# Four edits to the schedule of a two-layer graph and expert network: where a pair is added to X, which small loads come first, and the order of the first prologue

## The chip, the cores and the metric

The kernel runs on one core of a Trainium2 chip. The metric is the device time in microseconds (us). Before the change the median of three runs is 4302.01 us (4301.11 to 4304.52).

## The reference

Four residual layers work on x, 2048 rows of 128 channels. Every layer reads the row-normalised x and its result is added to x:

```python
x = x + _L0_gnn_ref(_layernorm(x), ...)   # masked attention over the graph, 8 heads of 16 channels, with a curvature bias
x = x + _L0_ffn_ref(_layernorm(x), ...)   # product keys: top 16 of a table for each row and head, then causal attention
x = x + _L1_gnn_ref(_layernorm(x), ...)   # graph attention:
#   Wh = einsum('nf,hfd->hnd', x, W_heads); e = leaky_relu(Wh.a1 [:, None] + Wh.a2 [None, :])
#   att = softmax(where(adj > 0, e, NEG)); feat = elu(att @ Wh) for 8 heads of 128; feat @ W_out + b_out
x = x + _L1_ffn_ref(_layernorm(x), ...)   # 16 experts, the best two by gate weighted, then a row norm
```

## The kernel before

X stays on the chip (16 tiles of 128 rows). Three stages follow one another, each with a barrier at its end; every engine has its own written-out instruction list and the order is set by semaphores alone.

**curvature_keys_and_attention** does the first two layers. A unit is 16 nodes with their 8 heads, a tile of X has 8 units. Its prologue loads some 30 constants through SP's queue (L421 to L452), normalises X, and makes `hT`, `vals` (L522, copied at L705), the two products with `al_w` and `ar_w` (L528, L532), `el_wide` (L709), `er_rows` (L712) and, on VectorE, `el_cols` (L838, L843). SP waits for `er_rows` (L440), stores it as the last rows of `bias_rhs` (L442), and then issues the loads of the key and attention weights (L443 to L452). TensorE waits for all of these before the first `logits_of` (L550). After that the units run: score matmuls, a maximum on VectorE (`max_of`, L862), exp on ScalarE (L732), four turns and products (L557, L565). One tile later the rows of the tile before choose their keys (`choose`, L905 to L966): 16 gathers a unit on GpSimd (L506), which VectorE adds two units later (L991). In the first unit with a choice (t = 1, k = 0) the order on TensorE is query product (L641), `logits_of` for the next unit, similarity product (L650); on ScalarE `qT` copy (L774), `relu_of`, `diff_of`, `sim` copy (L784); on VectorE `max_of`, then `choose`.

**graph_attention** is the third layer: 128 units u (8 heads of 16 tiles), and pairs g = u // 2 of two tiles of one head. VectorE makes the scores of the next unit (`scores`: L1394, L1398, L1404) and one reciprocal (L1443); ScalarE the exp of the next unit between the second and third of its four copies (L1331, L1340); TensorE turns the unit four blocks at a time (L1240) and lays the products of the pair before between them (`weigh`, L1253). At the end of every even unit 2m TensorE makes `project(m - 3)` (L1264). In VectorE's list an even turn 2m of the loop is: scores(2m + 1), reciprocal, `head_of(m - 2)` (L1412, L1415), `add_to_x(m - 3)` (L1431, waits for `project(m - 3)`). An odd turn 2m + 1 is: scores(2m + 2), reciprocal, `feat_of(m - 2)` (L1421, waits for `exp_below(m - 2)` of ScalarE, L1345, and for `project(m - 3)`). The reciprocals of a pair go through DRAM and come back on all partitions: two stores (L1186), a wait for both, one load (L1190), all on SP's queue in order. In head 0 VectorE also scales a tile of the mask in every unit (L1381); in four units of a head TensorE makes the values of the next head (L1219). The stage's prologue loads five constants on one semaphore; TensorE waits for all five, makes 16 products of one column each (L1198), and only then turns the normalised X (L150).

**experts** loads nine constants on one semaphore, turns X, waits for all nine, makes the gate products (L1546), chooses two experts on VectorE (L1635 to L1661), and runs 64 up and down products.

Of the kernel before, what the change touches and what calls it, by code (L numbers as in the profile page):

```python
# [7 lines left out]
P = 128  # L8
T = N // P
H = 8  # L10
CH = 512
# [179 lines left out]
def curvature_keys_and_attention(nc, ins, X, ident, big_ident, psL, psT, psV, psO, keysT_out, values_out, adj_out):  # L191
# [28 lines left out]
    with ExitStack() as ctx:  # L220
# [195 lines left out]
        with nc.Block() as block:  # L416
            @block.sync
            def _(sp):
# [33 lines left out]
                sp.dma_start(ahead[:, :], ins["c_ahead"][:, 0, 0:P]).then_inc(at_in, 16)  # L452

# [57 lines left out]
            def _(pe):  # L511
# [3 lines left out]
                for c in range(NC):  # L515
                    nc.tensor.matmul(psL[:, c * CH:(c + 1) * CH], w_t, xT[:, c * CH:(c + 1) * CH],
                                     start=True, stop=True).then_inc(prep_mm, 1)
                for q in range(4):
# [6 lines left out]
                pe.wait_ge(weights_ready, 2)  # L525
                pe.wait_ge(prep_copied, 8)
                for c in range(NC):
                    nc.tensor.matmul(psL[:, c * CH:(c + 1) * CH], al_w, hT[:, c * CH:(c + 1) * CH],  # L528
                                     start=True, stop=True).then_inc(prep_mm, 1)
                for c in range(NC):  # L530
                    pe.wait_ge(prep_copied, 9 + c)
                    nc.tensor.matmul(psL[:, c * CH:(c + 1) * CH], ar_w, hT[:, c * CH:(c + 1) * CH],  # L532
                                     start=True, stop=True).then_inc(prep_mm, 1)
# [97 lines left out]
                def tile(t, s1, last, choosing, adding):  # L631
                    for k in range(H):
# [10 lines left out]
                        if s1:  # L643
# [54 lines left out]
            def _(act):  # L698
                norm.scalar(act)
                for c in range(NC):  # L700
                    act.wait_ge(prep_mm, c + 1)
                    nc.scalar.copy(hT[:, c * CH:(c + 1) * CH], psL[:, c * CH:(c + 1) * CH]).then_inc(prep_copied, 1)
                for q in range(4):
                    act.wait_ge(prep_mm, 4 + q + 1)
                    nc.scalar.copy(vals[:, 4 * q:4 * q + 4, :].rearrange("p s c -> p (s c)"),  # L705
                                   psT[:, q % 2, :]).then_inc(prep_copied, 1)
                for c in range(NC):
                    act.wait_ge(prep_mm, 8 + c + 1)
                    nc.scalar.mul(el_wide[:, c * CH:(c + 1) * CH], psL[:, c * CH:(c + 1) * CH],  # L709
                                  1.0 - SLOPE).then_inc(prep_copied, 1)  # L710
                act.wait_ge(prep_mm, 16)
                nc.scalar.copy(er_rows[:, :], psL[:, :]).then_inc(prep_copied, 4)  # L712
                act.wait_ge(cols_ready, 2)
                act.wait_ge(prep_copied, 16)
# [53 lines left out]
                def tile(t, s1, last, choosing, adding):  # L768
                    for k in range(H):
                        v = H * (t - 1) + k  # L770
                        ahead = k < KU - 1 or not last
                        if choosing:
                            act.wait_ge(qT_done, v + 1)
                            nc.scalar.copy(qT[:, :], psT[:, 0, 0:P]).then_inc(qT_copied, 1)  # L774
                        if s1 and ahead:
# [3 lines left out]
                        if choosing:  # L779
# [36 lines left out]
                diff_of(0, 0)  # L816
# [7 lines left out]
            def _(dve):  # L824
# [12 lines left out]
                dve.wait_ge(prep_copied, 12)  # L837
                nc.vector.tensor_tensor(el_wide.rearrange("p (u i) -> p u i", i=G),  # L838
                                        el_wide.rearrange("p (u i) -> p u i", i=G),
                                        node_pick[:, :].unsqueeze(1).to_broadcast([P, UNITS, G]),  # L840
                                        ALU.mult).then_inc(el_mult, 1)
                dve.wait_ge(el_mult, 1)
                nc.vector.tensor_reduce(el_cols[:, :], el_wide.rearrange("p (u i) -> p u i", i=G),  # L843
                                        mybir.AxisListType.X, ALU.add).then_inc(cols_ready, 1)
# [166 lines left out]
                def tile(t, s1, last, choosing, adding):  # L1011
                    for k in range(H):
# [16 lines left out]
                        if s1 and ahead:  # L1029
# [9 lines left out]
                        else:  # L1039
                            attend_now()  # L1040
                        if summing is not None:
# [19 lines left out]
                turn_adj(0)  # L1061
                dve.wait_ge(keys_in, 64)
# [6 lines left out]
def graph_attention(nc, ins, X, ident, psL, psT, psV, psO, adj_kept, s2_kept, rinv_kept):  # L1069
# [9 lines left out]
    with ExitStack() as ctx:  # L1079
# [33 lines left out]
        consts_in = sem("consts_in")  # L1113
        adj_in = [sem(f"adj_in{g}") for g in range(4)]
# [41 lines left out]
        with nc.Block() as block:  # L1156
            @block.sync
            def _(sp):
                sp.dma_start(w_all[:, :], ins["W_all"]).then_inc(consts_in, 16)
                sp.dma_start(w_heads_t, ins["W_heads_t"]).then_inc(consts_in, 16)  # L1160
                sp.dma_start(a_cols, ins["a_cols"]).then_inc(consts_in, 16)
# [33 lines left out]
            def _(pe):  # L1195
                pe.wait_ge(consts_in, 80)
                for n in range(2 * H):
                    last = nc.tensor.matmul(psO[:, n:n + 1], w_heads_t[:, n % H, :], a_cols[:, n:n + 1],  # L1198
                                            start=True, stop=True)
# [31 lines left out]

                for c in range(NC):
# [132 lines left out]
            def _(dve):  # L1365
# [6 lines left out]
                def add_bias():  # L1372
# [425 lines left out]
```

## Time and profile before

| | |
|---|---|
| median of three runs | 4302.01 us |
| the profiled execution | 4302.53 us |
| its span, first to last instruction | 4300.8 us |
| busy over the span | PE 80%, VectorE 77%, ScalarE 53%, GpSimd 48% |
| mean granted TensorE clock | 0.919 of full speed |
| first stage, prologue and units | about 0 to 3002 us |
| graph attention | 3002 to 4034 us |
| experts | 4034 to 4300 us |

The profile names engines PE (matmul), PEld (weight load), DVE (VectorE), ACT (ScalarE), POOL (GpSimd) and SP (the DMA queue's engine). A line of the timeline has the start, the duration, the engine, the line of code, the operation, output and input with their shapes, how many instructions were merged, and in brackets how long the engine was idle before and what ended that. A matmul of 32-bit data shows as two instructions.

### The profile page before, as it was taken

How to read it: one execution, taken by the hardware profiler on the slowest of the kernel's cores; microseconds unless marked ns; L12 is line 12 of the kernel's file. 1: busy time of each engine (PE TensorE's matmuls, PEld its weight loads, DVE VectorE, ACT ScalarE, POOL GpSimd, SP SyncE). 2: the span in 40 equal slices, each digit the busy share in tenths (PEclk: the TensorE clock that was granted, in tenths of full speed). 3: DMA queues.
4: the chain of work that ended last, by engine and by line, in shares of the span. 5: the costliest groups of instructions: out<-in, count | busy, mean ns of one | idle time of the engine just before them, and what ended most of it. 6: DMA issues, size and time to landing. Idle time of an engine off the chain costs nothing. (4 is left out here: it accounts for less than half of the span.)

```text
span 4300.8 us, 61129 instructions
## 1 busy us (share of the span) xinstructions
PE 3427.1 (80%) x19161; PEld 2640.9 (61%) x19288; DVE 3315.0 (77%) x10546; ACT 2259.3 (53%) x3612; POOL 2047.6 (48%) x2052
## 2 busy tenths in 40 slices
PE   6867778777777788888888989665878888887799
PEld 4645555555555566666666666544667777776676
DVE  2679889898898898988988889774777777777434
ACT  5645455555555565565655656322555555555333
POOL 0377777777777777777767667661000000000000
PEclk9988889899999999999999999777899999999899
DMA  2244444455455555555556555553322122222200
GB/s 76 60 128 118 134 141 131 145 143 154 149 155 161 162 166 175 176 173 175 187 172 199 177 166 194 185 176 136 102 29 25 14 29 29 29 29 9 46 3 8
DMA packets 217422, 501.28 MB, mean 117 GB/s; under 512 B 63676, under 2 KB 115072, under 8 KB 210816
## 3 DMA queue, kind: packets, MB, share of 16 engines
q0 software_dynamic: 98304, 268.57, 21.4%
q1 hardware_dynamic: 118796, 228.80, 19.1%
q8 instruction: 156, 2.56, 0.3%
q14 instruction: 166, 1.36, 0.2%
HBM read 470.64 MB, written 26.41 MB: 116 GB/s over the span
## 5 line engine op out<-in xcount | busy, mean ns | idle before, releaser
L506 POOL DMA_INDIRECT ck_ring<-in_tables,ck_rows x2048 | 2047.4, 1000 | 884.0 <-issue 750.6
L991 DVE SCALAR_TENSOR_TENSOR ck_part<-ck_ring,ck_norm_w,ck_part 128x256 f32<-128x256 f32 x1792 | 770.0, 477 | 61.2 <-DVE ck_rows L966 41.7
L565 PE MATMUL psV<-ck_vals,ck_probsT 128*128 128x128 f32 x4096 | 556.5, 285 | 109.0 <-ACT ck_probsT L740 102.5
L550 PE MATMUL psL<-ck_bias_rhs,ck_bias_w 110*128 110x512 f32 x1024 | 573.4, 643 | 87.1 <-ACT ck_bias_rhs L727 38.5
L565 PEld LDWEIGHTS psV<-ck_vals,ck_probsT 128*128 128x128 f32 x4096 | 504.2, 197 | 157.8 <-ACT ck_probsT L740 89.0
L1253 PE MATMUL psL<-ga_probsT,ga_vals 128*128 128x256 f32 x2048 | 531.5, 407 | 0.7 <-ACT ga_probsT L1340 0.7
L740 ACT COPY ck_probsT<-psT 128x512 f32<-128x512 f32 x512 | 281.9, 587 | 446.4 <-PE psT L557 445.3
L1240 PE MATMUL psT<-ident,ga_probs 128*128 128x128 f32 x2048 | 300.2, 281 | 188.8 <-ACT ga_probsT L1340 187.6
L1253 PEld LDWEIGHTS psL<-ga_probsT,ga_vals 128*128 128x128 f32 x2048 | 399.5, 205 | 51.7 <-ACT ga_probsT L1340 0.9
L1240 PEld LDWEIGHTS psT<-ident,ga_probs 128*128 128x128 f32 x2048 | 248.3, 145 | 242.2 <-issue 214.5
L1331 ACT ACTIVATE ga_probs<-ga_probs,ga_neg_mx 128x2048 f32<-128x2048 f32 x128 | 256.4, 2003 | 225.4 <-DVE ga_neg_mx L1404 225.2
L1340 ACT COPY ga_probsT<-psT 128x512 f32<-128x512 f32 x512 | 280.3, 584 | 177.8 <-PE psT L1240 177.6
L583 PE MATMUL psL<-ck_keysT,ck_at_qT 128*128 128x512 f32 (+3 forms) x640 | 271.2, 556 | 91.0 <-DVE ck_neg_mx L866 90.9
L602 PE MATMUL psO<-ck_at_probsT,ck_values 128*128 128x128 f32 x2176 | 308.0, 291 | 41.5 <-ACT ck_at_probsT L747 41.5
L602 PEld LDWEIGHTS psO<-ck_at_probsT,ck_values 128*128 128x128 f32 x2176 | 276.1, 201 | 71.2 <-ACT ck_at_probsT L747 71.2
L550 PEld LDWEIGHTS psL<-ck_bias_rhs,ck_bias_w 110*128 110x128 f32 x1024 | 213.6, 209 | 166.4 <-issue 146.3
L557 PE MATMUL psT<-ident,ck_probs 128*128 128x128 f32 x2048 | 307.5, 286 | 3.1 <-ACT ck_sim L784 2.7
L1394 DVE SCALAR_TENSOR_TENSOR ga_probs<-ga_s_rows,ga_s_cols,ga_s_slope 128x2048 f32<-128x2048 f32 x128 | 300.3, 2346 | 0.6
L1398 DVE CUSTOM_DVE_ANT_0 ga_probs<-ga_probs,ga_adj_neg 128x2048 f32<-128x2048 f32 x128 | 292.7, 2286 | 5.5
L862 DVE CUSTOM_DVE_ANT_0 ck_relu_part<-psL,ck_relu_part 128x2048 f32<-128x2048 f32 x128 | 292.8, 2288 | 0.5 <-issue 0.5
L747 ACT COPY ck_at_probsT<-psT 128x512 f32<-128x512 f32 (+3 forms) x320 | 158.9, 524 | 206.0 <-PE psT L590 206.0
L732 ACT ACTIVATE ck_probs<-ck_relu_part,ck_neg_mx 128x2048 f32<-128x2048 f32 x128 | 257.8, 2014 | 16.0 <-DVE ck_neg_mx L866 16.0
(210 smaller groups left out, 5455.7 us busy)
## 6 DMA issues: line engine op xcount, KB each, us to landing
ck_ring<-in_tables,ck_rows POOLq DMA_INDIRECT x2048, 2.8
ck_adj_raw<-in_adj SPq DMA_DIRECT2D x16, 1024.0 KB, 9.0
adj_scratch<-ck_adj_neg SPq DMA_DIRECT2D x16, 512.0 KB, 10.4
values_scratch<-ck_values_tile SPq DMA_DIRECT2D x128, 64.0 KB, 1.7
keysT_scratch<-ck_keys_tile SPq DMA_DIRECT2D x128, 64.0 KB, 1.9
ck_keysT<-keysT_scratch SPq DMA_DIRECT2D x8, 1024.0 KB
ck_values<-values_scratch SPq DMA_DIRECT2D x8, 1024.0 KB
ga_adj_neg<-adj_scratch SPq DMA_DIRECT2D x16, 512.0 KB, 11.6
```

The source lines that it names most:

```text
L506: pool.indirect_dma_start(ring[:, slot, :], None, ins["tables"], bass.IndirectOffsetOnAxis(rows[:, k, s:s + 1], axis=0)).then_inc(got[(u * ...
L550: last = nc.tensor.matmul(psL[:, c * CH:(c + 1) * CH], bias_w[:, :], bias_rhs[:, k % 2, c * CH:(c + 1) * CH], start=False, stop=True)
L557: last = nc.tensor.transpose(psT[:, q % 2, s * P:(s + 1) * P], probs[:, j * P:(j + 1) * P], ident[:, :])
L565: last = nc.tensor.matmul(psV[:, k % 2, :], probsT[:, q % 2, s, :], vals[:, j, :], start=(j == 0), stop=(j == T - 1))
L602: last = nc.tensor.matmul(psO[:, P:2 * P], values[:, j, :], at_probsT[:, q % 2, j % 4, :], start=(j == 0), stop=(j == blocks(v) - 1))
L740: nc.scalar.copy(probsT[:, q % 2, :, :].rearrange("p s c -> p (s c)"), psT[:, q % 2, :]).then_inc(probsT_ready, 1)
L862: nc.vector.tensor_tensor_reduce(out=logits[:, :], in0=psL[:, :], in1=relu_part[:, :], scale=1.0, scalar=-3.0e38, op0=ALU.add, op1=ALU.max ...
L991: done.append(c.did(nc.vector.scalar_tensor_tensor(part[:, s % 2, :], ring[:, slot, :], norm_w[:, s:s + 1], part[:, s % 2, :], ALU.mult, A ...
L1240: last = nc.tensor.transpose(psT[:, q % 2, s * P:(s + 1) * P], probs[:, u % 3, j * P:(j + 1) * P], ident[:, :])
L1253: last = nc.tensor.matmul(out, vals[:, k % 2, j, :], probsT[:, g % 2, j, :, :].rearrange("p h i -> p (h i)"), start=(j == 0), stop=(j == T ...
L1394: nc.vector.scalar_tensor_tensor(probs[:, u % 3, :], s2_rows[:, k % 2, :], s1_cols[:, t, k:k + 1], s2_slope[:, k % 2, :], ALU.add, ALU.max ...
L1398: nc.vector.tensor_tensor_reduce(out=probs[:, u % 3, :], in0=probs[:, u % 3, :], in1=adj_neg[:, t, :], scale=1.0, scalar=-3.0e38, op0=ALU.add,
```

## The change

- **graph_attention, loop:** `add_to_x(m - 3)` moves from the even turn 2m to the odd turn 2m + 1, behind `feat_of(m - 2)`.
- **graph_attention, prologue:** the two loads for the score weights come first and have a semaphore of their own; the 16 products of one column become 8 of two columns. The other three loads are waited for before the first values, and before the bias is added.
- **experts:** the gate's weights, bias and numbering are loaded first, on their own semaphore; TensorE waits for the other six loads only after the gate products, VectorE before the gates.
- **First prologue:** the `al_w` and `ar_w` products come ahead of the `vals` products; ScalarE copies in that order and makes `diff_of(0, 0)` between the second and third copy of `vals`; SP's wait for `er_rows` and the two stores move behind the weight loads; VectorE turns the mask before it makes `el_cols`.
- **First unit with a choice:** the similarity product, its copy and `choose` come ahead of the logits, the relu and the maximum of the next unit.

```diff
@@ curvature_keys_and_attention, SP
-                sp.wait_ge(prep_copied, 13)
-                for b in range(2):
-                    sp.dma_start(bias_rhs[KW:KB, b, :], er_rows[0:H, :]).then_inc(er8_in, 16)
                 sp.dma_start(wq[:, :, :], ins["Wq_pk"]).then_inc(keys_in, 16)
...
                 sp.dma_start(ahead[:, :], ins["c_ahead"][:, 0, 0:P]).then_inc(at_in, 16)
+                sp.wait_ge(prep_copied, 12)
+                for b in range(2):
+                    sp.dma_start(bias_rhs[KW:KB, b, :], er_rows[0:H, :]).then_inc(er8_in, 16)
@@ TensorE: the two score products, then vals
+                pe.wait_ge(weights_ready, 2)
+                pe.wait_ge(prep_copied, 4)
+                for c in range(NC):
+                    nc.tensor.matmul(psL[...], al_w, hT[...], start=True, stop=True).then_inc(prep_mm, 1)
+                for c in range(NC):
+                    pe.wait_ge(prep_copied, 5 + c)
+                    nc.tensor.matmul(psL[...], ar_w, hT[...], start=True, stop=True).then_inc(prep_mm, 1)
                 for q in range(4):
-                    pe.wait_ge(prep_copied, 4 + q)
+                    if q >= 2:
+                        pe.wait_ge(prep_copied, 11 + q)
@@ TensorE, tile
+                        opening = choosing and not adding and k == 0
-                        if s1:
+                        if s1 and not opening:
                             if k < KU - 1:
                                 logits_of(t, k + 1)
...
+                        if opening:
+                            logits_of(t, k + 1)
@@ graph_attention
-                pe.wait_ge(consts_in, 80)
-                for n in range(2 * H):
-                    last = nc.tensor.matmul(psO[:, n:n + 1], w_heads_t[:, n % H, :], a_cols[:, n:n + 1],
-                                            start=True, stop=True)
+                pe.wait_ge(heads_in, 32)
+                both = a_cols.rearrange("f (a h) -> f h a", h=H)
+                for h in range(H):
+                    last = nc.tensor.matmul(psO[:, 0:2 * H].rearrange("c (a h) -> c h a", h=H)[:, h, :],
+                                            w_heads_t[:, h, :], both[:, h, :], start=True, stop=True)
...
-                    if u % 2 == 0 and 0 <= u // 2 - 3 < GROUPS:
+                    if u % 2 == 1 and 0 <= u // 2 - 3 < GROUPS:
                         add_to_x(u // 2 - 3)
@@ experts
-                pe.wait_ge(consts_in, 144)
+                pe.wait_ge(gate_in, 48)
                 pe.wait_ge(norm.xT_done, T // 4)
...
                 last.then_inc(gates_done, 1)
+                pe.wait_ge(consts_in, 96)
```

## Rows read from the trace of the kernel before

**Rows 1.** Windows, graph attention: length, then busy by engine, granted clock, DMA share.

```profile
3095.00:4017.00 922.00, 744.67 (x4272) 649.51 (x4272) 664.14 (x961) 538.30 (x808) 0.00 (x0) 0.94 0.23 25
3059.00:3112.00 53.00, 47.09 (x275) 38.42 (x273) 41.94 (x61) 34.37 (x55) 0.00 (x0) 1.00 0.32 35
```

**Rows 2.** Waits, 3100 to 4010: who waited for whom, total, times, longest.

```profile
DVE X L1431 <- PE psV L1264: 241.3, 59, 6.2
```

**Rows 3.** Timeline, graph attention, units 112 to 115.

```profile
3903.96 1.11 PE L1240 MATMUL psT<-ident,ga_probs 128*128 128x128 f32 x8 [2.76 <-ACT ga_probsT L1340]
...
3911.53 0.42 DVE L1431 TENSOR_TENSOR X<-X,psV 128x256 f32<-128x256 f32 x1 [4.74 <-PE psV L1264]
...
3911.81 1.06 PE L1240 MATMUL psT<-ident,ga_probs 128*128 128x128 f32 x8 [0.32 <-ACT ga_probsT L1340]
3911.86 2.35 DVE L1394 SCALAR_TENSOR_TENSOR ga_probs<-ga_s_rows,ga_s_cols,ga_s_slope 128x2048 f32<-128x2048 f32 x1
...
3917.11 2.35 DVE L1394 SCALAR_TENSOR_TENSOR ga_probs<-ga_s_rows,ga_s_cols,ga_s_slope 128x2048 f32<-128x2048 f32 x1
...
3919.97 1.06 PE L1240 MATMUL psT<-ident,ga_probs 128*128 128x128 f32 x8 [2.77 <-ACT ga_probsT L1340]
...
3922.50 0.29 DVE L1415 TENSOR_SCALAR ga_belowT<-ga_headT 128x256 f32<-128x256 f32 x1
...
3925.89 0.42 ACT L1345 ACTIVATE ga_belowT<-ga_belowT 128x256 f32<-128x256 f32 x1
3926.14 1.06 PE L1240 MATMUL psT<-ident,ga_probs 128*128 128x128 f32 x8 [0.32 <-ACT ga_probsT L1340]
```

**Rows 4.** Timeline: starts of units 3, 4, 7 and 127, mask scaling, values.

```profile
3062.86 1.06 PE L1240 MATMUL psT<-ident,ga_probs 128*128 128x128 f32 x8 [0.77 <-ACT ga_probsT L1340]
...
3069.02 1.06 PE L1240 MATMUL psT<-ident,ga_probs 128*128 128x128 f32 x8 [0.77 <-ACT ga_probsT L1340]
...
3069.60 0.69 DVE L1381 TENSOR_SCALAR ga_adj_neg<-ga_adj_neg 128x2048 bf16<-128x2048 bf16 x1
...
3088.47 1.04 PE L1240 MATMUL psT<-ident,ga_probs 128*128 128x128 f32 x8
...
3600.59 1.06 PE L1219 MATMUL psL<-ga_w_all,ga_xT 128*128 128x128 f32 x8
...
4017.12 1.06 PE L1240 MATMUL psT<-ident,ga_probs 128*128 128x128 f32 x8 [0.32 <-ACT ga_probsT L1340]
```

**Rows 5.** L1186 (the store), then tile ga_rinv_rows (the load): issue to landing.

```profile
DMA to landing us min/median/max: 7.2/8.7/12.1
...
DMA to landing us min/median/max: 3.8/4.9/8.6
```

**Rows 6.** First prologue: timeline; last row: a load of 0 to 110, us to landing.

```profile
22.93 1.16 PE L522 MATMUL psT<-ck_ring,ck_at_probs 128*128 128x128 f32 x8 [0.68 <-ACT ck_relu_part L702]
...
30.36 3.67 PE L528 MATMUL psL<-ck_relu_part,ck_ring 128*128 128x512 f32 x8 [0.77 <-ACT ck_vals L705]
...
37.56 1.87 ACT L712 COPY ck_er_rows<-psL 128x2048 f32<-128x2048 f32 x1 [2.90 <-PE psL L532]
...
53.29 1.91 PE L550 MATMUL psL<-ck_bias_rhs,ck_bias_w 110*128 110x512 f32 x2 [15.83 <-DMA ck_ahead<-in_c_ahead]
...
ck_wq<-in_Wq_pk SPq DMA_DIRECT2D x1, 512.0 KB, 4.4
```

**Rows 7.** Timeline, first unit with a choice and the first wait for gathers.

```profile
151.41 0.27 ACT L774 COPY ck_qT<-psT 128x128 f32<-128x128 f32 x1 [0.58 <-PE psT L641]
...
158.29 0.48 DVE L905 MAX8 ck_best<-ck_sim 128x8 f32<-128x128 f32 x2
...
200.88 1.67 DVE L991 SCALAR_TENSOR_TENSOR ck_part<-ck_ring,ck_norm_w,ck_part 128x256 f32<-128x256 f32 x4 [2.89 <-DMA ck_ring<-in_tables,ck_rows]
```

**Rows 8.** Timeline, graph attention's prologue: the products of the score weights.

```profile
3012.00 6.99 PE L1198 MATMUL psO<-ga_probs 128*128 128x1 f32 x32 [11.73 <-DMA ga_b_out<-in_b_out]
```

**Rows 9.** Timeline, experts: the gate products.

```profile
4048.71 7.01 PE L1546 MATMUL psO<-ex_gate_w,ex_xT 128*128 128x16 f32 x32 [4.26 <-DMA ex_expert_no<-in_c_expert_no]
```

More of the change, by code:

```diff
@@ L524, in _ @@
                     last.then_inc(prep_mm, 1)
[L525 to L533, printed above, removed]
                 def logits_of(t, k, first=False):
@@ L702, in _ @@
                     nc.scalar.copy(hT[:, c * CH:(c + 1) * CH], psL[:, c * CH:(c + 1) * CH]).then_inc(prep_copied, 1)
+                for c in range(NC):
+                    act.wait_ge(prep_mm, 4 + c + 1)
+                    nc.scalar.mul(el_wide[:, c * CH:(c + 1) * CH], psL[:, c * CH:(c + 1) * CH],
+                                  1.0 - SLOPE).then_inc(prep_copied, 1)
+                act.wait_ge(prep_mm, 12)
+                nc.scalar.copy(er_rows[:, :], psL[:, :]).then_inc(prep_copied, 4)
                 for q in range(4):
-                    act.wait_ge(prep_mm, 4 + q + 1)
+                    act.wait_ge(prep_mm, 12 + q + 1)
                     nc.scalar.copy(vals[:, 4 * q:4 * q + 4, :].rearrange("p s c -> p (s c)"),
                                    psT[:, q % 2, :]).then_inc(prep_copied, 1)
[L707 to L712, printed above, removed]
+                    if q == 1:
+                        act.wait_ge(cols_ready, 1)
+                        nc.scalar.activation(bias_rhs[0:KC, 0, :], c_rows[:, :], ACT.Relu, bias=c_cols[:, 0:1]
+                                             ).then_inc(diff_ready, 1)
                 act.wait_ge(cols_ready, 2)
-                act.wait_ge(prep_copied, 16)
+                act.wait_ge(prep_copied, 12)
                 def relu_of(t, k):
@@ L774, in tile @@
                             nc.scalar.copy(qT[:, :], psT[:, 0, 0:P]).then_inc(qT_copied, 1)
+                        opening = choosing and t == 1 and k == 0
+                        if opening:
+                            act.wait_ge(sim_done, v + 1)
+                            act.wait_ge(sim_free, v + 1)
+                            nc.scalar.copy(sim[:, k % 2, :, :].rearrange("p a b -> p (a b)"),
+                                           psT[:, 1, 0:2 * NK]).then_inc(sim_copied, 1)
                         if s1 and ahead:
@@ L778, in tile @@
                             diff_of(t, k + 2)
-                        if choosing:
+                        if choosing and not opening:
                             act.wait_ge(sim_done, v + 1)
@@ L1028, in tile @@
                             pick(t, k - 1)
-                        if s1 and ahead:
+                        opening = choosing and not adding and k == 0
+                        if s1 and ahead and not opening:
                             max_of(t + (k + 1) // KU, (k + 1) % KU)
@@ L1040, in tile @@
                             attend_now()
+                        if opening:
+                            max_of(t, k + 1)
                         if summing is not None:
@@ L1061, in _ @@
                 turn_adj(0)
+                dve.wait_ge(prep_copied, 8)
+                nc.vector.tensor_tensor(el_wide.rearrange("p (u i) -> p u i", i=G),
+                                        el_wide.rearrange("p (u i) -> p u i", i=G),
+                                        node_pick[:, :].unsqueeze(1).to_broadcast([P, UNITS, G]),
+                                        ALU.mult).then_inc(el_mult, 1)
+                dve.wait_ge(el_mult, 1)
+                nc.vector.tensor_reduce(el_cols[:, :], el_wide.rearrange("p (u i) -> p u i", i=G),
+                                        mybir.AxisListType.X, ALU.add).then_inc(cols_ready, 1)
                 dve.wait_ge(keys_in, 64)
@@ L1230, in piece @@
                         values(k, c, c % 2)
+                pe.wait_ge(consts_in, 48)
                 for c in range(NC):
@@ L1501, in experts @@
         consts_in = sem("consts_in")
+        gate_in = sem("gate_in")
         gates_done = sem("gates_done")
```

28 lines of the change are left out of this document (13 added, 15 removed).

## The prediction

> **What bounds the kernel now.** I read the windows by stage first, then the waits of the longest stage that the change touches, then its timeline, then the starts of the three stages. In graph attention no engine is full: of 922 us TensorE is busy 745 and VectorE 664, and the granted clock is 0.94 on average [rows 1]. So the loop hangs on waits. The largest one is VectorE's: 241.3 us in 59 waits at `add_to_x` for `project` [rows 2]. The timeline shows why this wait counts [rows 3]. A pair lasts from one odd turn's start to the next, 3911.81 to 3926.14, 14.33 us. TensorE projects at the end of an even unit; VectorE stands at L1431 until then (4.74 us here), and begins the scores of 2m + 2 only at 3911.86, when TensorE is already in the odd unit 2m + 1. Those scores need 5.25 us (3911.86 to 3917.11), their exp follows, the third and fourth copy of the odd unit queue behind that exp on ScalarE, and TensorE idles 2.77 us before it may start unit 2m + 2 at 3919.97. The odd unit takes 8.16 us. The even unit behind it, whose exp was ready in time, takes 6.17 (3919.97 to 3926.14) though it holds the projection. In other pairs the clock falls after the idle time and the even unit takes 7.85 (3903.96 to 3911.81), so that such a pair lasts 16.0.
>
> The three stages begin with loads and small products during which nothing else runs: TensorE waits 15.83 us before the first logits [rows 6], 11.73 before the score weights [rows 8], 4.26 before the gates [rows 9].
>
> **The change part by part, against the profiled execution of 4302.53 us** (1.7 us more than its span, 0.5 more than the median).
>
> *add_to_x one turn later.* No instruction is added. The add now stands behind `feat_of`, which waits for the same projection and for ScalarE's small exp. That exp ends at 3925.89 + 0.42, 0.2 us after the odd unit's start [rows 3]. So VectorE again stands still until the even unit's end; queued behind are the add and the scores of 2m + 3, no longer those of 2m + 2, which are done by then. What is late next? VectorE's own pair: 5.25 for an odd turn, 5.4 + 0.2 for an even one (3917.11 to 3922.50, and the start of what follows), 0.35 for the add, 11.2 us. Counted from an odd start plus 0.2: feat and add to 0.9, scores of 2m + 3 and head to 6.5, scores of 2m + 4 to 11.4. The exp of 2m + 3 is wanted after the first two copies of unit 2m + 2, some 2 us into it, at about 8; that of 2m + 4 at about 14. Both are early. So TensorE's chain binds: turns, products, last copy. Its unit lasts 6.17 in the even case above, and 6.16 in an odd unit early in the loop, before any add (3062.86 to 3069.02 [rows 4]). A pair becomes 12.3 us, with 1.1 us to spare on VectorE.
>
> Now the sum from unit 7 to unit 127, which is 3088.47 to 4017.12, 928.7 us [rows 4]. Head 0 has nine of these units and one more VectorE instruction of 0.69 in each [rows 4]: 11.2 + 1.4 = 12.6 a pair, 6.3 a unit, 57 us. The other 111 units at 6.16 are 684. In four units of six heads TensorE also makes values, 1.06 us [rows 4], of which the 0.77 that TensorE idles at each unit's end hides most: 24 times about 0.4, 10 us (between 0 and 25). Together 751, a gain of **177 us** (165 to 185).
>
> The reciprocals' way through DRAM must keep up. From the reciprocal of unit 2g + 1 to `head_of(g)` the new order leaves about 19 us (a pair of 12.3, 6 us into the unit that follows, 1 us before the pair). Store and load take 8.7 + 4.9 at the median, 12.1 + 8.6 at worst [rows 5], with 0.5 for issues: 14 to 21. So a rare stall of 2 us, which the spare 1.1 a pair gives back.
>
> *Score weights first.* The 32 instructions of 6.99 us become 16, 3.5 less for certain [rows 8]. They wait for two loads instead of five. The nearest row for a 512 KB load at the head of a queue is 4.4 us [rows 6], against the 11.73 of idle time here; 0.4 for the second issue and 2 us more for its small packets, and 4.2 of waiting go. If the five loads land together anyhow, none goes. Gain **7.7** (3.5 to 8.5). The loads that now come later are wanted only after four score chunks.
>
> *Gate loads first.* TensorE idles 4.26 [rows 9]; the last copy of xT, about 0.6, stays in front. Gain **3.6** (2 to 5). VectorE still waits for the six big loads, now issued 1.4 us later; they were in by 4048.7 and the gates end at about 4052, which hides them.
>
> *First prologue.* The `al_w` products can start where the `vals` products do now, 22.93. From their start to the end of the `er_rows` copy it takes 30.36 to 39.43, 9.07 us [rows 6], so `er_rows` is there at 32.0. Behind it ScalarE makes four copies of 512 columns and one `diff` of 2048, which by the 1.87 of the 2048-column copy are about 0.6 and 1.9: 36.3. The store of `er_rows` is issued at 32.0, two issues take about 1.5, and it lands 4.4 later by the nearest row: 37.9. The weight loads, no longer behind that wait, are issued from about 21 on. So the first logits start near 37.9 instead of 53.29, 15.4 us earlier; if the store needed as long as the loads behind it do now (39.43 to 53.29), at 45.9, 7.4 earlier. The products ran at half clock, 1.91 for two, after the 15.83 of idling; with a short idle time up to 3 us more. Gain **18** (7 to 20). SP's wait now holds back the next tile's mask load, which is wanted 100 us later. All that follows starts so much earlier.
>
> *First choice.* `choose` starts at 158.29 behind the maximum; its query is copied by 151.68 [rows 7]. The similarity product and its copy still lie between (about 1.1 us): gain 5.5, between a loss of 1 (the next unit's relu, exp and maximum queue behind the choice) and 6.6. It counts as far as gathers are late, and they are: VectorE waits 2.89 for them two units on [rows 7]. **5.5**.
>
> Sum 177 + 7.7 + 3.6 + 18 + 5.5 = 211.8, so 4302.5 - 211.8 = 4090.7 us, say 4091; by all bounds 4077 to 4126.
>
> **The rivals.** *The clock keeps falling.* Half of the even units now cost 7.85 - 6.16 = 1.7 more after a slow-clock stretch [rows 3]. If the 0.77 of idling that stays at each unit's end is enough for that, 60 pairs keep half of 1.7, 51 us: 4142. Against it: the stretch 3059 to 3112, mostly units of 6.2 with just that idling, is granted 1.00 [rows 1]. The Trainium skill's page "TensorE: Matmul & The Clock Gate", section "A second HAM failure mode: psum-queue depth-cycling", says that many short waits between groups of matmuls can make the clock go up and down; by that rule the time would be this rival's, and the stretch at 1.00 does not bear it out. Chance 0.14.
>
> *The wait only moves.* If `feat_of` holds VectorE so that a pair stays at 14.33 [rows 3] and only the slow-clock stretches go, the loop gains 928.7 - 60 x 14.33 = 69: 4302.5 - 69 - 35 = 4199. For it: VectorE's wait is there as before. Against it: what stands behind it is wanted a unit later. Chance 0.06.
>
> *The loop gains nothing*, because something that the waits do not show ends last, and only the four starts gain 34.8: 4268. Chance 0.05.
>
> *Slower: the way through DRAM binds.* If the first store of a pair must land before the second and both before the load, a pair costs 8.7 + 8.7 + 4.9 = 22.3 [rows 5] instead of 15.5, 60 x 6.8 = 408 more, 4676 in all. It decides as soon as this chain is longer than a pair. Against it: the chain fits in two turns now and a store does not seem to wait for the one before it. Chance 0.03.
>
> **How the numbers follow.** The forecast, 4091, has 0.70, the slow clock 0.14, the moved wait 0.06, no gain in the loop 0.05, slower 0.03, and 0.02 is left for no change that can be measured. A measurement of this kernel can tell 0.2%, 8.6 us, from no change. The range goes from the lower bound of the sum to just beyond the slow-clock case, 4076 to 4150; the other cases, 0.16, and some of the tails are left out. Faster 0.95, within 0.2% 0.02, slower 0.03.
>
> **What would show it.** In the profile of the changed kernel the 241 us of L1431 should be gone and a wait of about 1 us a pair appear at L1421; units of L1240 should start every 6.2 us, odd and even; the granted clock over the loop should be near 1.00; the exp at L1331 should no longer wait for L1404. The first L550 should start near 38, L1198 near 3012 - 24 - 4 = 2984 with half as many instructions, L1546 right behind the last xT copy, the first gather 24 us earlier. The forecast is wrong if L1412 waits for the reciprocals' load in every pair, if VectorE is without idle time in heads 1 to 7, or if the clock still falls every second pair.

## The result and the profile of the changed kernel

The changed kernel takes **4089.54 us** (median of four runs, 4084.63 to 4093.33) against 4301.56 us for the kernel before (4298.51 to 4304.52, four runs). The ratio is 0.951, with an interval of 0.9495 to 0.9525. The forecast was 4091.0, in a range of 4076 to 4150. Its profiled execution took 4088.79 us with a span of 4087.0, so 213.8 us less span than before.

The page's head and engine rows, with the share of the span in brackets:

```profile
span 4087.0 us, 61096 instructions
...
PE 3365.6 (82%) x19145; PEld 2594.8 (63%) x19272; DVE 3311.8 (81%) x10546; ACT 2248.0 (55%) x3612; POOL 2051.7 (50%) x2052
```

Where the span's 213.8 us went, read from the starts in the two timelines:

| piece | before, us | after, us | difference |
|---|---|---|---|
| start to the first maximum of the scores | 60.11 | 48.83 | -11.3 |
| first maximum to first gather | 106.94 | 101.50 | -5.4 |
| first gather to the start of graph attention | 2835.3 | 2836.9 | +1.6 |
| its start to the first turn of unit 0 | 38.44 | 28.54 | -9.9 |
| unit 0 to unit 7 | 47.7 | 47.5 | -0.2 |
| unit 7 to unit 127 | 928.6 | 745.0 | **-183.6** |
| unit 127 to the start of experts | 17.55 | 17.97 | +0.4 |
| experts | 266.1 | 260.7 | -5.4 |

Of what was changed, the third row has only the next unit's maximum and exp, which now come behind `choose`. It went from 2833.5 to 2842.2 in the ten executions profiled for this study, so a step there of some 4 us between two executions means nothing. The starts differ too: in the other profiles of the changed kernel's opening (the two pads and `split_wait`, below) the first maximum came at 46.3 to 46.6, so the 11.3 of this pair is a low one.

The loop first. The windows view has the stretch's length, the busy time of each engine (PE, PEld, DVE, ACT, POOL), the granted clock, the share of the DMA engines and GB/s, as in [rows 1]:

```profile
3064.00:3808.00 744.00, 695.11 (x4301) 616.25 (x4299) 662.47 (x962) 530.33 (x810) 0.00 (x0) 1.00 0.28 32
```

The clock is 1.00 over all of it, where it was 0.94 [rows 1]. TensorE is now busy 93% of the stretch, VectorE 89%, with the same VectorE work (662 us against 664). The waits from 3070 to 3800 (who waited for whom, total, times, longest) take the place of [rows 2]:

```profile
ACT ga_probsT L1359 <- PE psT L1259: 200.3, 206, 1.2
PEld psT L1259 <- issue: 64.5, 89, 1.0
DVE ga_featT L1441 <- ACT ga_belowT L1364: 63.6, 55, 2.0
PE psT L1259 <- ACT ga_probsT L1359: 48.1, 89, 0.8
```

The 241.3 us of VectorE at `add_to_x` are gone. What is left is 63.6 at `feat_of`, 1.16 each time. The largest row is now ScalarE waiting for TensorE's turns, the reverse side of a TensorE that is nearly full. The timeline shows one pair, to be held against [rows 3]:

```profile
3703.53 1.06 PE L1259 MATMUL psT<-ident,ga_probs 128*128 128x128 f32 x8 [0.77 <-ACT ga_probsT L1359]
...
3705.21 2.02 ACT L1350 ACTIVATE ga_probs<-ga_probs,ga_neg_mx 128x2048 f32<-128x2048 f32 x1
...
3708.76 0.61 PE L1283 MATMUL psV<-ga_w_out,ga_featT 128*128 128x128 f32 x4
...
3709.45 0.42 ACT L1364 ACTIVATE ga_belowT<-ga_belowT 128x256 f32<-128x256 f32 x1
3709.69 1.06 PE L1259 MATMUL psT<-ident,ga_probs 128*128 128x128 f32 x8 [0.32 <-ACT ga_probsT L1359]
3709.90 0.43 DVE L1441 SCALAR_TENSOR_TENSOR ga_featT<-ga_belowT,ga_headT 128x256 f32<-128x256 f32 x1 [1.10 <-ACT ga_belowT L1364]
3710.24 0.41 DVE L1451 TENSOR_TENSOR X<-X,psV 128x256 f32<-128x256 f32 x1
3710.57 2.34 DVE L1414 SCALAR_TENSOR_TENSOR ga_probs<-ga_s_rows,ga_s_cols,ga_s_slope 128x2048 f32<-128x2048 f32 x1
...
3715.86 0.41 PE L1259 MATMUL psT<-ident,ga_probs 128*128 128x128 f32 x2 [0.77 <-ACT ga_probsT L1359]
```

Units start 6.16 and 6.17 us apart. The add (L1451) stands behind `feat_of` (L1441) at the odd unit's start, and the scores behind both (3710.57) belong to a unit that is wanted a whole unit later. The two idle times left on TensorE, 0.77 and 0.32, are its wait for ScalarE's last copy.

The starts. First the opening: the issue of the two stores of `er_rows`, the first logits, the `al_w` products, the copy of `er_rows`, the first `choose`, the first gather; then the score weights and the gates, to be held against [rows 6 to 9]:

```profile
24.99 3.67 PE L521 MATMUL psL<-ck_relu_part,ck_ring 128*128 128x512 f32 x8 [0.77 <-ACT ck_relu_part L706]
...
32.19 1.86 ACT L712 COPY ck_er_rows<-psL 128x2048 f32<-128x2048 f32 x1 [2.90 <-PE psL L525]
...
34.08 1.50 SPq L452 DMA_DIRECT2D ck_bias_rhs<-ck_er_rows  x2
...
42.40 1.91 PE L551 MATMUL psL<-ck_bias_rhs,ck_bias_w 110*128 110x512 f32 x2 [5.75 <-ACT ck_bias_rhs L735]
...
141.58 0.49 DVE L910 MAX8 ck_best<-ck_sim 128x8 f32<-128x128 f32 x2 [2.72 <-ACT ck_sim L787]
...
150.33 1.08 POOL L506 DMA_INDIRECT ck_ring<-in_tables,ck_rows  x1 [149.88 <-issue]
...
2990.74 3.57 PE L1216 MATMUL psO<-ga_probs 128*128 128x2 f32 x16 [5.59 <-DMA ga_probs<-in_a_cols]
...
3836.67 5.29 PE L1567 MATMUL psO<-ex_gate_w,ex_xT 128*128 128x16 f32 x32 [0.77 <-ACT ex_xT L141]
```

The first logits wait for the stores (issued at 34.08), the loads and the first `diff` (ScalarE made it from 34.91 to 36.92). The releaser that the row names, L735, is the second `diff`, which was still running at 42.40. In the profile of `vector_pad_small`, with the same prologue, it ran on until 41.93 while the first product had begun at 39.98, so the product does not wait for it; what came last is a transfer.

### The profile page after: what moved, and what is told of

The parts are those of the page before. It is cut to its first block and busy times, and to the rows that moved or that the text cites. A ratio compares the mean times of both kernels' runs of the same rounds, so it can differ in the third digit from the quotient of the medians.

```text
span 4087.0 us, 61096 instructions
## 1 busy us (share of the span) xinstructions
PE 3365.6 (82%) x19145; PEld 2594.8 (63%) x19272; DVE 3311.8 (81%) x10546; ACT 2248.0 (55%) x3612; POOL 2051.7 (50%) x2052
## 5 line engine op out<-in xcount | busy, mean ns | idle before, releaser
L1272 PE MATMUL psL<-ga_probsT,ga_vals 128*128 128x256 f32 x2048 | 484.9, 380 | 0.7 <-ACT ga_probsT L1359 0.7
L1272 PEld LDWEIGHTS psL<-ga_probsT,ga_vals 128*128 128x128 f32 x2048 | 370.5, 191 | 40.2 <-ACT ga_probsT L1359 0.9
L1259 PE MATMUL psT<-ident,ga_probs 128*128 128x128 f32 x2048 | 292.0, 276 | 60.4 <-ACT ga_probsT L1359 59.1
L1259 PEld LDWEIGHTS psT<-ident,ga_probs 128*128 128x128 f32 x2048 | 240.1, 142 | 107.2 <-issue 79.7
L591 PE MATMUL psT<-ident,ck_at_probs 128*128 128x128 f32 x1088 | 175.0, 296 | 106.7 <-ACT ck_keys_tile L808 98.4
```

Of the source, the lines that this page charges most:

```text
L1259: last = nc.tensor.transpose(psT[:, q % 2, s * P:(s + 1) * P], probs[:, u % 3, j * P:(j + 1) * P], ident[:, :])
L1272: last = nc.tensor.matmul(out, vals[:, k % 2, j, :], probsT[:, g % 2, j, :, :].rearrange("p h i -> p (h i)"), start=(j == 0), stop=(j == T ...
```

## Experiments

All ratios are to the kernel before. Beside the first four experiments (1 to 4) it took 4302.15 us (seven runs, 4296.59 to 4306.75), beside the last four (5 to 8) 4301.07 (nine runs, 4294.9 to 4303.96).

**1. One line.** `add_alone` is the kernel before with the loop's edit and nothing else.

```diff
-                    if u % 2 == 0 and 0 <= u // 2 - 3 < GROUPS:
+                    if u % 2 == 1 and 0 <= u // 2 - 3 < GROUPS:
                         add_to_x(u // 2 - 3)
```

> The kernel before with one edit: add_to_x stands in the odd turn behind feat_of. Theory (VectorE's wait for the projection delayed the next scores, and with them the exp, the copies and TensorE): units of the loop start every 6.16 us, odd and even, as in the changed kernel, and the time falls by 184 us, to about 4118. Rival (the loop gains only together with the other edits, or those carry a good part of the 212): a fall of less than 150 us.

Measured: 4114.89 us (4109.62 to 4120.17), ratio 0.9561, interval 0.9545 to 0.9577. The loop takes 745.1 us, with the clock at 1.00. Its waits have the row of the full change under the old line number:

```profile
DVE ga_featT L1421 <- ACT ga_belowT L1345: 63.2, 54, 2.0
```

So this line carries 187 of the 212 us between the medians; 183.5 of them lie between units 7 and 127.

**2. How much of it is the clock?** The line takes away both a wait and TensorE's 2.8 us of idle time before every even unit, behind which the clock fell in half the pairs [rows 3]. `idle_filled` keeps the wait and fills most of the idle time with transposes that nothing reads.

```diff
                     if half == 0 and 0 <= m - 3 < GROUPS:
                         project(m - 3)
+                    if half == 1 and 2 <= g and u < UNITS - 1:
+                        for _ in range(16):
+                            nc.tensor.transpose(psO[:, 0:P], ident[:, :], ident[:, :])
```

> The kernel before with 16 transposes of the identity at the end of every odd unit, about 2.1 us of work in the 2.77 us in which TensorE idles there; nothing reads them and add_to_x stays where it was. Theory (half of the pairs last 16.0 instead of 14.33 because the clock falls after the idle time): the clock stays at 1.00, all pairs last 14.3, time about 4233, 69 us less, though work is added. The remaining 115 us of the loop's gain would then be the wait itself. Rival (the falls have another cause): pairs of 16.0 stay, time about 4302 or more.

Measured: 4251.59 us (4245.53 to 4254.65), ratio 0.9878, interval 0.9861 to 0.9894. The loop takes 875.2 us, 53.4 less than before. Windows of the loop, waits and timeline of this kernel:

```profile
3100.00:3960.00 860.00, 788.64 (x5182) 708.71 (x5182) 658.74 (x953) 527.61 (x798) 0.00 (x0) 1.00 0.23 27
```

```profile
DVE X L1434 <- PE psV L1264: 189.6, 59, 4.0
```

```profile
3902.68 1.91 PE L1294 MATMUL psO<-ident 128*128 128x128 f32 x16
...
3905.62 1.07 PE L1240 MATMUL psT<-ident,ga_probs 128*128 128x128 f32 x8 [1.02 <-ACT ga_probsT L1343]
...
3911.78 1.06 PE L1240 MATMUL psT<-ident,ga_probs 128*128 128x128 f32 x8 [0.32 <-ACT ga_probsT L1343]
...
3919.94 1.07 PE L1240 MATMUL psT<-ident,ga_probs 128*128 128x128 f32 x8 [1.02 <-ACT ga_probsT L1343]
```

Units last 6.16 and 8.16 us: every pair is the 14.33 us pair of [rows 3], none the slower one. In the kernel before, the trace has 31 stretches at half clock in this loop, 109 us together (the 0.94 of [rows 1] over 922 us says the same); here there is none. So of the 183.6 us about 53 are the clock's and, by difference, 130 the wait's. The expectation of 69 left out the units with values (8.64 here) and head 0, where the odd units last 9.37.

**3 and 4. How much room does VectorE have?** Two kernels add to the changed one a VectorE instruction per pair that nothing reads, behind the add: `vector_pad_small` a memset, `vector_pad_large` an addition.

```diff
                         add_to_x(u // 2 - 3)
+                        if u // 2 > 3:
+                            dve.wait_ge(spared, u // 2 - 3)
+                        nc.vector.memset(spare[:, :], 0.0).then_inc(spared, 1)
```

> The changed kernel with one more VectorE instruction a pair in graph attention, a memset of 1024 columns behind add_to_x (about 0.9 us). Theory (TensorE's chain of 6.16 a unit binds, VectorE waits 1.16 us a pair at feat_of): units stay at 6.16 in heads 1 to 7, the time rises by 0 to 6 us (head 0, where VectorE has nothing to spare). Rival (VectorE binds too): 0.9 a pair more, about 53 us.

```diff
+                nc.vector.memset(spare[:, :], 0.0).then_inc(spared, 1)
                 scores(0)
...
                         add_to_x(u // 2 - 3)
+                        if True:
+                            dve.wait_ge(spared, u // 2 - 2)
+                        nc.vector.tensor_tensor(spare[:, :], spare[:, :], spare[:, :], ALU.add).then_inc(spared, 1)
```

> The changed kernel with a larger VectorE instruction a pair behind add_to_x, an addition of 1920 columns (about 2.1 us). Theory (1.16 us a pair to spare): 2.1 - 1.16 = 1.0 a pair more in heads 1 to 7 and 2.1 in head 0, about 65 us in all. Rival (VectorE has much more to spare): under 20 us. Rival (it binds already): 2.1 a pair, about 128 us.

Measured: 4088.98 and 4144.14 us, one run each. The loops take 747.2 (+2.2, all of it in head 0) and 799.0 (+54.0, where 65 were expected). The added instruction and the wait that shows its effect, of the small pad:

```profile
L1475 DVE MEMSET ga_spare<- x64: 912/912/912, 3062.2 to 3824.7; 128x1024 f32 x64
```

```profile
DVE ga_featT L1443 <- ACT ga_belowT L1366: 8.3, 12, 1.0
```

and of the large one:

```profile
L1476 DVE TENSOR_TENSOR ga_spare<-ga_spare x64: 2150/2152/2155, 3061.3 to 3876.7; 128x1920 f32<-128x1920 f32 x64
```

```profile
ACT ga_probs L1352 <- DVE ga_neg_mx L1426: 165.7, 118, 3.4
```

The small pad, 0.91 us a pair, is taken out of VectorE's wait almost whole: 63.6 - 8.3 = 55.3 us, and 60 times 0.912 is 54.7. Of the large pad's 2.15 a pair, 54.0 / 60 = 0.90 reaches the time, so 1.25 were free. ScalarE's exp then waits for VectorE's maxima, a row that is not among the large waits of the changed kernel. Both say the same: VectorE had some 1.2 us a pair to spare, and TensorE's chain set the pace.

**5. Which part of the opening?** `loads_order_alone` takes from the change only SP's order (the wait for `er_rows` and its stores behind the weight loads) and the score weights' loads first, with the 16 products of one column kept. The products of the prologue stay in the old order.

```diff
-                sp.wait_ge(prep_copied, 13)
-                for b in range(2):
-                    sp.dma_start(bias_rhs[KW:KB, b, :], er_rows[0:H, :]).then_inc(er8_in, 16)
                 sp.dma_start(wq[:, :, :], ins["Wq_pk"]).then_inc(keys_in, 16)
...
+                sp.wait_ge(prep_copied, 13)
+                for b in range(2):
+                    sp.dma_start(bias_rhs[KW:KB, b, :], er_rows[0:H, :]).then_inc(er8_in, 16)
...
+                sp.dma_start(w_heads_t, ins["W_heads_t"]).then_inc(heads_in, 16)
+                sp.dma_start(a_cols, ins["a_cols"]).then_inc(heads_in, 16)
                 sp.dma_start(w_all[:, :], ins["W_all"]).then_inc(consts_in, 16)
...
```

> The kernel before with two edits alone: SP's wait for er_rows and its two stores stand behind the weight loads (the products keep their old order), and the two loads for the score weights come first with their own wait (still 16 products of one column). Theory for the first prologue (the wait in SP's queue held the weight loads back; now the stores of er_rows land last, and they land late wherever they stand): first logits near 44.5 us instead of 53.3, so that this edit brings most of the 10.9 us and the order of the products only some 2. Rival (the products' order brings most): first logits not before 48. Theory for the score weights: from the stage's first load to the first turn of unit 0 about 32 us (38.5 before, 28.6 in the changed kernel), the rest being the halved products. Rival (the loads land together anyhow): 35 or more.

Measured: 4295.12 us, one run. The timeline's rows for the stores' issue, the first products behind them, and the score weights' products:

```profile
41.69 1.51 SPq L452 DMA_DIRECT2D ck_bias_rhs<-ck_er_rows  x2
...
46.73 0.59 PE L546 MATMUL psL<-ck_adj_neg,ck_spread 128*128 128x512 bf16 x1 [7.03 <-DMA ck_bias_rhs<-ck_er_rows]
...
3005.03 6.99 PE L1199 MATMUL psO<-ga_probs 128*128 128x1 f32 x32 [5.45 <-DMA ga_probs<-in_a_cols]
```

The first L550 started at 47.11, against 53.29 before, though in this execution the `al_w` products began later, 32.60 against 30.36. From `al_w` to the first logits it is 14.51 against 22.93, so SP's order alone saves 8.4 us. Counted from the start of the run, the first logits lie between the theory's 44.5 and the rival's 48; 2.2 of the 2.6 us to the theory are the later start. In the changed kernel the order of the products adds the rest: its `al_w` products start 5.4 us earlier than before, of which 2.9 go again in a longer way from there to the logits (17.41), and 8.4 + 5.4 - 2.9 is the 10.9. Here the named release is the store's landing, 5.0 us after its issue, with all loads ahead of it landed. Graph attention's start to unit 0 took 31.89. With the 6.99 us of products unhalved, that is 6.5 less than in the profile of before. But `add_alone`, with the old prologue, took 33.32, so the sum alone does not show the gain; TensorE's idle time does, 5.45 here against 10.76 to 11.73 in three profiles of the old order. The loop is that of the kernel before: 928.9 us, again 109 us of them at half clock.

**6. Do the weight loads delay the stores?** `stores_before_weights` is the changed kernel with the stores issued ahead of the three attention loads, whose wait on TensorE moves to the first tile that needs them.

```diff
-                sp.dma_start(at_wq[:, :, :], ins["Wq"]).then_inc(at_in, 16)
-                sp.dma_start(at_wo[:, :, :], ins["Wo"]).then_inc(at_in, 16)
-                sp.dma_start(ahead[:, :], ins["c_ahead"][:, 0, 0:P]).then_inc(at_in, 16)
                 sp.wait_ge(prep_copied, 12)
                 for b in range(2):
                     sp.dma_start(bias_rhs[KW:KB, b, :], er_rows[0:H, :]).then_inc(er8_in, 16)
+                sp.dma_start(at_wq[:, :, :], ins["Wq"]).then_inc(at_in, 16)
+                sp.dma_start(at_wo[:, :, :], ins["Wo"]).then_inc(at_in, 16)
+                sp.dma_start(ahead[:, :], ins["c_ahead"][:, 0, 0:P]).then_inc(at_in, 16)
...
                 def tile(t, s1, last, choosing, adding):
+                    if t == 1:
+                        pe.wait_ge(at_in, 48)
...
                 pe.wait_ge(keys_in, 64)
-                pe.wait_ge(at_in, 48)
```

> The changed kernel, but the stores of er_rows stand ahead of the three attention-weight loads in SP's queue, and TensorE waits for those three loads only before tile 1, where they are first used. Theory (in the changed kernel the stores are issued at 34 but land near 42 because the loads ahead of them fill the queue): first logits at about 38.5 to 39 instead of 42.4, first maximum near 45 instead of 48.8. Rival (the stores need those 6 to 8 us by themselves): first logits stay at 41 or later.

Measured: 4081.02 us, one run. The stores' issue and the first product behind them:

```profile
32.31 1.49 SPq L449 DMA_DIRECT2D ck_bias_rhs<-ck_er_rows  x2
...
37.57 0.38 PE L547 MATMUL psL<-ck_adj_neg,ck_spread 128*128 128x512 bf16 x1 [2.69 <-DMA ck_bias_rhs<-ck_er_rows]
```

The first logits came at 37.78, 4.6 us earlier than in the changed kernel's profile, but part of that is an earlier start of the `al_w` products (23.22 against 24.99). From the stores' issue to the first logits it takes 5.47 us here, 5.53 in experiment 8, which has the same order, and 5.42 in `loads_order_alone`. With the three loads just ahead of the stores it takes 8.32 in the changed kernel (34.08 to 42.40), 7.58 in `split_wait`, and 6.01 and 5.64 in the two pads. What differs among these four is when the last of the loads ahead, `ahead`, landed. In the changed kernel it was issued at 30.07 and took 10.2 us:

```profile
30.07 1.29 SPq L449 DMA_DIRECT2D ck_ahead<-in_c_ahead  x1
...
DMA to landing us min/median/max: 10.2/10.2/10.2
```

So it landed at 40.3, in the other three at 37.9 to 38.1, and in all four the first logits follow 1.7 to 2.3 us later. By this the loads ahead of the stores cost 0.1 to 2.9 us, the more the later they land behind the stores' issue (3.5 to 6.2 us). That is one profile for each of seven kernels: a cost that goes with the landing of the loads is shown, its usual size is not.

**7. What bounds the loop now?** By the timeline TensorE waits 0.77 or 0.32 us at each unit's start for the fourth copy of the unit before, though its first four turns write the bank that the third copy has already emptied. `split_wait` is the changed kernel with that wait in two.

```diff
                         if u >= 1:
-                            pe.wait_ge(probsT_ready, 4 * u)
+                            pe.wait_ge(probsT_ready, 4 * u - 1)
                         turn(u, 0)
+                        if u >= 1:
+                            pe.wait_ge(probsT_ready, 4 * u)
                         turn(u, 1)
```

> The changed kernel with TensorE's wait at the start of a unit split: the first four turns wait for the third copy of the unit before, only the next four for the fourth. Theory (TensorE's chain of turns, products and last copy binds, with 0.77 us of idling a unit for the last copy, and VectorE's pair of 11.2 us is next): units fall from 6.16 to about 5.7 in heads 1 to 7, 111 times 0.45, 50 us less, about 4040. Rival (ScalarE's or VectorE's part of the chain binds already): units stay at 6.1 or more, time within 10 us of the changed kernel.

Measured: **4041.4 us** (five runs, 4038.1 to 4045.81), ratio 0.9398, interval 0.9386 to 0.9411. The loop takes 698.8 us, 46.2 less than the changed kernel's. Windows, waits and timeline of this kernel:

```profile
3030.00:3720.00 690.00, 679.52 (x4237) 603.29 (x4236) 657.86 (x955) 524.40 (x802) 0.00 (x0) 1.00 0.28 34
```

```profile
DVE ga_featT L1443 <- ACT ga_belowT L1366: 15.3, 18, 1.4
...
ACT ga_probs L1352 <- DVE ga_neg_mx L1426: 5.3, 10, 0.8
...
DVE ga_headT L1434 <- DMA ga_rinv_rows<-rinv_scratch: 1.2, 3, 0.6
```

```profile
3600.58 0.66 PE L1259 MATMUL psT<-ident,ga_probs 128*128 128x128 f32 x4 [0.24 <-ACT ga_probsT L1361]
...
3605.86 1.05 PE L1259 MATMUL psT<-ident,ga_probs 128*128 128x128 f32 x8
...
3610.64 1.04 PE L1259 MATMUL psT<-ident,ga_probs 128*128 128x128 f32 x8
3611.91 0.66 PE L1259 MATMUL psT<-ident,ga_probs 128*128 128x128 f32 x4 [0.24 <-ACT ga_probsT L1361]
```

Two units now take 11.33 us (3600.58 to 3611.91), and VectorE's pair was worked out at 11.2 ahead of the change. That is the second sign of the chain: shortened by its last wait, the loop shortens. What stopped it at 11.33 is not shown. VectorE is busy 657.9 of 690 us, 95%, near the sum that was worked out for it; but TensorE is busy 679.5, 98%, and ScalarE's exp waits for VectorE only ten times. Both engines are full at about this length, and no run lengthens one of them alone.

**8. Both.** `split_wait_and_stores` joins the edits of 6 and 7.

> Both of the last two edits in one kernel. Theory: they lie in different stages and add up, about 50 and 4 us less than the changed kernel, about 4036. Rival (the earlier start is given back later in the first stage): the same time as with the split wait alone.

Measured: 4037.03 us (five runs, 4032.94 to 4038.7), ratio 0.9384, interval 0.9371 to 0.9397; the first logits at 37.86 and the loop at 698.8. It is the fastest kernel of this study, 52.5 us under the changed kernel's median. The 4.4 us to `split_wait` lie within what the two intervals leave open.

## Why the prediction was right, step by step

**The loop: right in its mechanism and nearly in its size.** The forecast was 177 us for units 7 to 127, in bounds of 165 to 185; it is 183.6. Every sign asked for in the loop is there: no wait at the add (L1451 here, L1431 before), 1.16 us a pair at `feat_of` (forecast 1.1), units every 6.2, clock 1.00, no large wait of the exp for VectorE. Two terms were too high. Head 0 was priced at VectorE's 6.3 a unit; its units go at TensorE's pace like all others, 6.13 to 6.6, and its nine took 56.3 us instead of 57: the pace was priced 1.3 too high, and the values in four of these units, which the term left out, took 0.9. The values were priced at 0.4 in each of 24 units; the trace has 6.57 in the even ones and 6.13 in the odd ones, so half of them cost nothing, 5 us less. The rest of the 751 stands.

**What the forecast did not separate** is how the gain divides. `idle_filled` puts about 53 us on the clock and, by difference, 130 on the wait. The prediction's moved-wait rival reckoned 69 for the clock, which missed by the same slips as the expectation of that run.

**The rivals.** *The clock keeps falling* is refuted: 1.00 over 744 us, although 0.77 and 0.32 us of idle time are left at the units' starts. The Trainium skill's page "TensorE: Matmul & The Clock Gate", section "A second HAM failure mode: psum-queue depth-cycling", says that frequent short idle times of TensorE between groups of matmuls made the clock swing in one kernel; the trace of this loop does not agree, since its short waits came every 6.2 us with no fall. *The wait only moves* is refuted by the pair of 12.33 us, *the loop gains nothing* by `add_alone`. *The way through DRAM binds* did not happen: the changed kernel waits 0.3 us for it in the whole loop, and even in the quicker loop of `split_wait` it is 1.2 us in three waits. Its trip is unchanged, store and load in the changed kernel (compare [rows 5]):

```profile
DMA to landing us min/median/max: 6.3/8.4/12.2
```

```profile
DMA to landing us min/median/max: 3.7/5.0/8.9
```

**The first prologue: right in direction, too large.** Forecast 18 us (7 to 20), measured 10.9 at the first logits and 11.3 at the first maximum. Over the profiles that have the one opening or the other (three old, four new) the first maximum moved from 60.9 to 47.0 on average, 13.9 us: the forecast is too large by that too. Of the 4.5 us between the forecast first logits (37.9) and the measured ones (42.40), 2.1 are the start of the `al_w` products. It was taken over as 22.93, and was 24.99 in this execution, 22.95 to 25.5 in others. The traces show where the 2.1 us go: to the eight products that make `hT`. They start at nearly the same time in both kernels, in the kernel before

```profile
18.56 3.70 PE L516 MATMUL psL<-ck_at_probs,ck_ring 128*128 128x512 f32 x8 [0.68 <-ACT ck_at_probs L141]
```

and in the changed one

```profile
18.68 5.55 PE L516 MATMUL psL<-ck_at_probs,ck_ring 128*128 128x512 f32 x8 [0.67 <-ACT ck_at_probs L141]
```

They follow each other at 0.43 us in the first, and in the second at 0.85 until 22.25, a factor of two as between the two levels of the clock. In five of the ten profiles they take 3.70, in the other five 5.55 to 6.06, with the old opening and with the new. So the price of 22.93 came from a fast execution. From the start of `al_w` to the end of the `er_rows` copy it takes 9.06 us (24.99 to 34.05), as priced. The other 2.4 are the stores: priced at 5.9 from that end to the logits by a load's 4.4, they took 8.35, between that price and the other that the prediction gave (to 45.9). In `stores_before_weights` the forecast's 37.9 was met (37.78), with an early start of `al_w`. The rest of the miss is the clock bonus of up to 3 us, which did not come: the first two products still took 1.91, as in [rows 6]. TensorE had idled 5.75 us before them, and the clock had fallen at 39.5; in `stores_before_weights`, after 2.69 us, they took 1.14. `loads_order_alone` shows that SP's order was 8.4 of the gain, near the 8.8 that its expectation gave it.

**Score weights: mis-sized by 2.2, which the spread of this piece covers.** Forecast 7.7 (3.5 to 8.5), measured 9.9. The products halved as priced, 6.99 to 3.57. The wait fell further: TensorE's idle time went from 11.73 [rows 8] to 5.59, where 7.5 was reckoned. The reckoning has a slip, since its own terms (4.4, 0.4 and 2) leave 4.9 of the 11.73 to gain and not 4.2, and its 2 us for small packets are in no row: both loads landed 3.1 us after their issue, the large one and the one of small packets. The piece as a whole also varies. With the old prologue it took 38.44, 36.46 and 33.32 us in the profiles of before, `idle_filled` and `add_alone`, with the new one 28.5 in five profiles and 30.46 in one. By the means that is 7.2, and a single difference of this stage is good to some 5 us.

**Gates: 5.4 against 3.6** (2 to 5). The wait shrank as forecast, 4.26 to 0.77 behind the last copy of xT. The rest is the clock, which was at its upper level for the first of the products: 5.29 us in place of 7.01 [rows 9]. In `split_wait` it was not, they took 6.98, and the gain was 3.5.

**First choice: 5.4 against 5.5.** `choose` and with it the first gather came earlier by what was worked out. In all profiles that have the edit the gather comes 101.5 to 102.6 us behind the first maximum, in those without it 106.9 to 110.7.

**So the sum, 211.8 forecast and 213.8 measured, hides errors that cancel:** the four starts were forecast at 34.8 and gave 32.0 (11.3 + 5.4 + 9.9 + 5.4), the loop was forecast 6.6 too low, and 1.8 went against it in stretches that the change hardly touches. That the sum came out within 2 us is luck. The part that carried the forecast is the loop; the small terms were known to about 5 us each. Two signs asked for in the starts are missing by this: the first gather came 16.7 us earlier and not 24, and the products of the score weights at 2990.7 and not near 2984.

**Left open:** why the clock rises about 5 us later in some executions than in others, with the same work on TensorE before it (from 13.5 to 13.8 us on), why the loads of the opening landed 2 us later in the changed kernel's profile than in three others, and which engine sets the 11.33 us of `split_wait`.

## What to carry to other kernels

When an engine with a written-out order waits long for another, ask what is queued behind the waiting instruction and when that is wanted: here the add could wait, the scores behind it could not, and moving one line by a turn was worth 187 us, with the wait cut from 241 to 63 us. After such a move add up each engine's own work for one turn of the loop: the larger sum here (12.3 for TensorE's chain) gave the new time. Once the next wait was split, the pair took 11.33, near VectorE's sum of 11.2, though there TensorE is as full. An idle time that repeats in a loop can cost a second time through the clock, so price it with and without the fall.

## What the runs showed of the hardware

- **The clock.** With 2.8 us of TensorE idle in every pair of 14.3 us the granted clock fell 31 times in 60 pairs, to half, for 3.5 us each on average (109 / 31). With 1.9 us of that time filled by transposes that nothing reads, and 1.02 left idle, it fell in none. Filling an idle time that was not removed gained 53 us in the loop (50.6 between the medians).
- **Stores from issue to use.** From the issue of the two stores of `er_rows`, 64 KB each, to the logits that need them it was 5.4 to 5.5 us in three executions where the weight loads stood behind them or had landed. Behind 1 MB of weight loads still under way it was 5.6, 6.0, 7.6 and 8.3 us, the logits 1.7 to 2.3 us behind the landing of the last load. The store of 128 values to DRAM in the loop lands after 6.3 to 12.2 us, the load that spreads them after 3.7 to 8.9.
- **Starts differ between executions.** The same instructions ahead of the first unit of graph attention took 33.32 to 38.44 us. The clock's changes fall at different places in them: the eight products that set `psO` from `ga_wa` took 1.87 us in the profile of before and 1.06 in that of `add_alone`. The loop behind them repeats to 0.1 us (745.0 and 745.1).
